# Filler matmuls, packed step places and one warm-up token less in a chunked sigmoid recurrence

## The reference, cut to what matters

```python
# x: (32, 32, 16, 25).  Three stages, each of them once:
# 1. a graph convolution with four temporal branches and a residual
# 2. attention over T*V = 400 tokens of 32 channels, per sample of the batch of 32
#    scores = exp(-(|q|^2 + |k|^2 - 2 q.k)); attn = softmax(scores); out = attn @ V, added to its input
# 3. a recurrence over the 400 tokens:
Wx = ((flat - mean) * rsqrt(var + 1e-5) * gamma + beta).reshape(B, T, H)    # H = 32
def step(yt, wx_t):
    yt = sigmoid(wx_t + yt @ V.T)            # V is orthogonal, 32 x 32
    return (yt, yt)
_, ys = scan(step, zeros(B, H), swapaxes(Wx, 0, 1))                          # 400 steps; ys is added to the input
```

## Time and profile before

| what | value |
|---|---|
| median of three runs | 237.83 us (237.7 to 238.28) |
| the profiled execution: its own time | 237.66 us |
| its span, first to last instruction | 235.8 us |
| PE busy | 199.2 us, 85% |
| ACT busy | 169.9 us, 72% |
| DVE busy | 157.7 us, 67% |
| mean granted TensorE clock | 0.956 |

### The profile page before, as it was taken

The page is one execution under the profiler, slowest core; times in us unless marked ns, Lnnn a source line. Parts: engine busy times, 40 slices in busy tenths (PEclk is TensorE's granted clock), DMA queues, the critical chain, the costliest instruction groups (busy, mean ns, idle before and its releaser), DMA issues. The chain is left out here.

```text
span 235.8 us, 3561 instructions
## 1 busy us (share of the span) xinstructions
PE 199.2 (85%) x1110; PEld 94.1 (40%) x1110; DVE 157.7 (67%) x296; ACT 169.9 (72%) x309; POOL 27.5 (12%) x44
## 2 busy tenths in 40 slices
PE   0775998898899797959989999999999998588950
PEld 0552554464465353523333343434343333245630
DVE  0417618965992992399578577777869695595880
ACT  4028179579759959797998999999899984365640
POOL 6000000054024006016100101010101000000000
PEclk9997699999999999997999999999999999889985
DMA  6940020039599709348880716162520000000016
GB/s 173 372 126 0 0 72 1 0 77 348 160 273 285 221 0 308 129 138 296 212 215 0 192 23 190 22 169 47 176 37 0 3 0 0 0 3 0 0 51 233
DMA packets 26883, 26.83 MB, mean 114 GB/s; under 512 B 1550, under 2 KB 25806, under 8 KB 26740
## 3 DMA queue, kind: packets, MB, share of 16 engines
q1 hardware_dynamic: 26868, 26.64, 38.6%
HBM read 14.74 MB, written 11.88 MB: 113 GB/s over the span
## 5 line engine op out<-in xcount | busy, mean ns | idle before, releaser
L474 ACT ACTIVATE arena<-ps 128x800 f32<-128x800 f32 (+1 forms) x56 | 44.5, 796 | 6.5 <-PE ps L980 4.9
L481 ACT ACTIVATE arena<-arena 128x800 f32<-128x800 f32 (+1 forms) x56 | 46.3, 829 | 0.0
L980 PE MATMUL ps<-qa,ka 128*128 128x400 bf16 (+1 forms) x128 | 35.8, 343 | 3.6 <-ACT arena L474 3.6
L980 PE MATMUL ps<-qb,kb 96*128 96x400 bf16 (+1 forms) x128 | 35.7, 341 | 0.0
L702 DVE TENSOR_TENSOR psum<-arena 128x400 f32<-128x400 f32 x32 | 19.6, 612 | 13.5 <-ACT arena L481 13.4
L702 DVE TENSOR_TENSOR psum<-psum,arena 128x400 f32<-128x400 f32 x32 | 19.5, 609 | 7.2 <-ACT arena L481 5.8
L1013 PE MATMUL ps<-arena,vb 128*32 128x400 f32 x192 | 21.0, 513 | 0.8 <-issue 0.8
L905 PE MATMUL ps<-arena,cst 128*128 128x400 f32 x32 | 15.7, 620 | 6.5 <-DVE arena L627 6.5
L980 PEld LDWEIGHTS ps<-qa,ka 128*128 128x128 bf16 (+1 forms) x128 | 10.4, 98 | 26.9 <-ACT arena L474 10.0
L1094 PE MATMUL ps<-yb,cst 128*128 128x160 f32 x76 | 17.2, 335 | 2.2 <-ACT yb L551 1.3
L711 DVE RECIPROCAL arena<-ps 128x400 f32<-128x400 f32 x7 | 18.6, 2651 | 0.0
(11 more groups left out here) (137 smaller groups left out, 357.4 us busy)
## 6 DMA issues: line engine op xcount, KB each, us to landing
dka<-arena SPq DMA_DIRECT2D x16, 200.0 KB, 3.1
dqa<-arena SPq DMA_DIRECT2D x16, 200.0 KB, 3.2
ka<-dka SPq DMA_DIRECT2D x8, 400.0 KB
qa<-dqa SPq DMA_DIRECT2D x8, 400.0 KB
arena<-x_tok SPq DMA_DIRECT2D x4, 400.0 KB
t<-x SPq DMA_DIRECT2D x1, 1600.0 KB, 12.1
dkb<-arena SPq DMA_DIRECT2D x8, 200.0 KB, 3.5
dqb<-arena SPq DMA_DIRECT2D x8, 200.0 KB, 4.6
```

The costliest lines, as they stand in the source:

```text
L474: nc.scalar.activation(prob[par][:, lo:hi, :], ps[:, o:o + hi - lo, 0:N], ACT.Exp, scale=2.0).then_inc(e1_done, 1)
L481: nc.scalar.activation(p, p, ACT.Exp).then_inc(p_ready, 1)
L980: last = mm_(ps[row:row + keys, bank, 0:N], kk[par][0:rows, b, o:o + keys], qq[par][0:rows, b, :], start=first, stop=not first, skip_group ...
```

## The change

Five things are changed.

1. A matmul `fill` of 256 bfloat16 columns into an unused bank (bank 3) follows every half step on TensorE, in both sweeps, and ten of them (`FILLS_FIRST`) stand between the last `prime` and the first half step.
2. Sweep 0 starts at token 1 of each chunk (`SKIP` = 1) and so takes nine steps.
3. The first of these nine has no matmul (its start state is zero), and ScalarE computes it straight from `ul` in SBUF, with `scl` and `shf` as scale and bias.
4. The steps' places are packed into banks 0 to 2 of each half (`PLACES` = 9): sweep 0 uses eight places, seeded as 3, 3 and 2; sweep 1 uses nine, and its last step takes place 0 again, seeded while the sweep runs (`last_seeds`). Six banks are primed and not eight. The signs of `tot` and `nshf` are turned (`shf`).
5. SP's loops over stores and loads are written out, and the loads of group 2 stand before the last `de` store.

```diff
-BLOCKS = ((0, 1), (1, 4), (4, 7), (7, 10))
+PLACES = 9
+SKIP = 1
+FILL = 256
+FILLS_FIRST = 10
...
-        PRIME_ORDER = (3, 7, 0, 4, 1, 5, 6, 2)
+        PRIME_ORDER = (0, 4, 1, 5, 2, 6)
+        FILL_BANK, SMALL_BANK = 3, 7
...
+        def place(sweep, s):
+            return s - SKIP - 1 if sweep == 0 else s % PLACES
...
-            with sp.Fori(1, PAIRS) as i:
+            for i in range(PAIRS - 1):
                 store(i)
-            with sp.Fori(1, PAIRS) as i:
-                for par in range(2):
-                    sp.wait_ge(s_done, UNITS * (2 * i + par - 1))
-                    load_operands(i, par)
+                store_e(i)
+                if i == 0:
+                    for par in range(2):
+                        load_operands(0, par)
+            store(PAIRS - 1)
+            load_next(1, 0)
+            store_e(PAIRS - 1)
+            load_next(1, 1)
+            for i in range(2, PAIRS):
+                for par in range(2):
+                    load_next(i, par)
...
             for h in range(2):
-                act.wait_ge(seeded[h], 1)
-                step(h, 0)
-            for s in range(1, L):
+                act.wait_ge(bn_c, 5)
+                nc.scalar.activation(y_half(h, SKIP + 1), ul[:, h, SKIP, :, :].rearrange("p g c -> p (g c)"),
+                                     ACT.Sigmoid, bias=shf, scale=scl).then_inc(y_ok[h], 1)
+            for s in range(SKIP + 1, L):
...
+            def last_seeds(base):
+                for h in range(2):
+                    dve.wait_ge(y_ok[h], base + 3)
+                    seed(h, 1, PLACES, L)
...
                 for j in range(L - 1):
+                    if seeding and j == 3:
+                        last_seeds(base)
...
+            def fill():
+                mm_(ps[:, FILL_BANK, 0:FILL], ka[0][:, 0, 0:P], ka[0][:, 0, 0:FILL], start=True, stop=True)
...
-            for bank in PRIME_ORDER[:-1]:
+            for bank in PRIME_ORDER:
                 prime(bank)
-            pe.wait_ge(bn_pe, 2)
-            prime(PRIME_ORDER[-1])
+            for _ in range(FILLS_FIRST):
+                fill()
...
+            def step(h, sweep, s):
+                mm_(step_slot(h, place(sweep, s)), c_("vT"), y_half(h, s), start=False, stop=True,
                     skip_group_check=True).then_inc(pre[h], 1)
+                fill()
```

More of the change, by code:

```diff
@@ L217, in build, with step_slot, seed_count @@
         LAST_BANKS = {G - 2: (0, 1), G - 1: (2, 3)}
-        def step_slot(h, s):
-            bank, o = (3, 0) if s == 0 else ((s - 1) // 3, SLOT * ((s - 1) % 3))
-            return ps[:, 4 * h + bank, o:o + SLOT]
-        def block_of(s):
-            return next(n for n, (lo, hi) in enumerate(BLOCKS) if lo <= s < hi)
+        def place(sweep, s):
+            return s - SKIP - 1 if sweep == 0 else s % PLACES
+        def step_slot(h, p):
+            return ps[:, 4 * h + p // 3, SLOT * (p % 3):SLOT * (p % 3 + 1)]
+        def seed_count(sweep, s):
+            return s // 3 + 1 + (PLACES // 3 + 1) * sweep - 1 if sweep else (s - SKIP - 1) // 3 + 1
         def y_half(h, s):
@@ L548, in _ @@
             nc.scalar.preload_act_table_set("sigmoid_and_others")
-            def step(h, s):
-                nc.scalar.activation(y_half(h, s + 1), step_slot(h, s), ACT.Sigmoid).then_inc(y_ok[h], 1)
+            def step(h, sweep, s):
+                nc.scalar.activation(y_half(h, s + 1), step_slot(h, place(sweep, s)), ACT.Sigmoid).then_inc(y_ok[h], 1)
             def steps(base):
@@ L571, in _ @@
                 with act.Fori(0, NC - 1) as k:
-                    steps(2 * L + L * k)
+                    steps(2 * L - SKIP + L * k)
         @block.vector
@@ L840, in _ @@
             with dve.If(dve.value_load(flag[0:1, 0:1], min_val=0, max_val=1) != 0):
-                dve.wait_ge(primed, len(PRIME_ORDER) + 1)
                 with dve.Fori(0, NC - 1) as k:
                     for h in range(2):
-                        chain(h, 2 * L + L * k)
-                        for n in range(len(BLOCKS)):
-                            seed(h, n)
+                        chain(h, 2 * L - SKIP + L * k)
+                        for lo, hi in LATER:
+                            seed(h, 1, lo, hi)
+                    last_seeds(2 * L - SKIP + L * k)
                 for h in range(2):
-                    dve.wait_ge(y_ok[h], 2 * L + L * (NC - 1))
+                    dve.wait_ge(y_ok[h], 2 * L - SKIP + L * (NC - 1))
                 dve.wait_ge(out_done, 16 * (G // OUT_G))
-                add_residual(2 * L + L * (NC - 2))
+                add_residual(2 * L - SKIP + L * (NC - 2))
         @block.tensor
@@ L1103, in steps @@
                         else:
-                            pe.wait_ge(y_ok[h], L * sweep + s)
-                        step(h, s)
-            for s in range(1, L):
+                            pe.wait_ge(y_ok[h], L * sweep - SKIP + s)
+                        step(h, 1, s)
+            for s in range(SKIP + 1, L):
                 for h in range(2):
-                    pe.wait_ge(seeded[h], block_of(s) + 1)
-                    pe.wait_ge(y_ok[h], s)
-                    step(h, s)
+                    pe.wait_ge(seeded[h], seed_count(0, s))
+                    pe.wait_ge(y_ok[h], s - SKIP)
+                    step(h, 0, s)
             steps(1)
             pe.wait_ge(cmp_c, 4)
-            mm_(ps[0:1, 7, 0:1], okc, c_("ones")[:, 0:1], start=True, stop=True).then_inc(cmp_pe, 1)
+            mm_(ps[0:1, SMALL_BANK, 0:1], okc, c_("ones")[:, 0:1], start=True, stop=True).then_inc(cmp_pe, 1)
             pe.wait_ge(flag_ok, 1)
             with pe.If(pe.value_load(flag[0:1, 0:1], min_val=0, max_val=1) != 0):
-                prime(7)
                 with pe.Fori(0, NC - 1) as k:
```

65 lines of the change are left out of this document (33 added, 32 removed).

## The result

| | before | changed |
|---|---|---|
| median of 20 executions each, same chip | 238.36 us (235.88 to 241.1) | 235.66 us (232.77 to 240.32) |
| ratio, 95% interval | | 0.987 (0.984 to 0.990) |
| the profiled execution: own time, span | 237.66, 235.8 | 235.07, 233.2 |
| mean granted clock in it | 0.956 | 0.967 |

The change is worth about 2.7 us by the medians (238.36 - 235.66), where 0.9 was forecast.

What follows compares the result with a forecast made beforehand. Taken as bound: the recurrence's latency, one half alternating matmul and sigmoid, 0.995 us a step. Own time 237.66 - 0.75 (start) - 0.1 (SP's queue) = 236.8; the median 0.17 above, less rounding: 236.9 us, range 236.0 to 237.8.

Steps and rivals of the forecast that it cites:

- term 2: SP's queue, at ScalarE's two waits for the last `dqb` store: written-out stores land slightly earlier, -0.1 us.
- the row nearest to the new form is not shorter: SP's stores: pair 0, already written out, took 7.33 us against 7.15 for looped pair 2, so little gain was booked.
- one of the two waits vanishes: ScalarE's waits for `dqb`: one disappears, -1.2 us; part of the more-is-gained rival, 236.0 us, 13%.
- term 1: Start of the recurrence: a step less (0.995), of which fills take back 0.25; -0.75 us.
- I take the phase that the trace shows: Start of the recurrence: clock assumed to rise at about 208.23, as in the one profiled execution; basis of -0.75 us.
- the ten fills booked as a cost: Between primes and first half step: ten fills set the start; they and the fill between halves take back 0.25 us.
- the prediction's bound of 1.7: Start of the recurrence: if the clock rises early, VectorE's seeds decide and the gain is up to -1.7 us.
- Rival 4: Recurrence steps: the fill's weight load is not hidden, steps take 1.17 us, 18 steps add 3.1; 240.0 us, 12%.
- Rival 2: Start of the recurrence: ten fills and some first steps run at half clock, leaving 0.16 of the gain; 237.6 us, 15%.
- the loop fills cost nothing at the upper level: Both sweeps: 36 fills stand in TensorE's idle time behind half steps, costed at nothing; cover 0.16 us a gap.
- the late seeds of step 9: Sweep 1 on VectorE: two seeds, 0.88 us, fit into 1.6 us of idle time; cost 0.
- nine steps meet the bound without further sweeps: Sweep 0: nine steps shrink a difference to 2^-18, just the comparison's bound; further sweeps, 388 us, given under 1%.

Runs made afterwards that it cites:

- e9: Changed kernel with 14 unused semaphore increments in SP's queue between pair 2's two sets of stores, delaying its last store; 237.14 us, ratio 0.988 to the kernel before.
- e7: Changed kernel with the last `de` store put back ahead of the loads of group 2; 236.98 us, ratio 0.995 to the kernel before.
- e11: Kernel before with 26 fills in TensorE's idle time ahead of the small matmul, nothing else changed; 238.17 us, ratio 0.998.
- e2: Changed kernel with the old SP queue of the kernel before; 236.77 us, ratio 0.993 to the kernel before.
- e1: Kernel before with the new written-out SP program alone; 237.36 us, ratio 0.990.
- e10: Changed kernel with three semaphore increments moved from the head of SP's program to GpSimd; 235.03 us, ratio 0.989 to the kernel before.
- e6: Changed kernel with 26 fills ahead of the small matmul instead of ten behind the primes, and the usual fills behind half steps; 235.13 us, ratio 0.987.
- e13: Changed kernel with SP's program three increments shorter and without any fill; 236.96 us, ratio 0.999 to the kernel before.
- e16: Kernel before with the written-out SP program, three increments shorter, and its old recurrence without fills; 236.76 us, ratio 0.993.
- e14: Changed kernel with SP's program three increments shorter and only the ten fills ahead of the first half step; 235.67 us, ratio 0.989 to the kernel before.
- e8: Changed kernel once more, unedited, beside three other runs on their chip; 236.72 us, ratio 0.994 to the kernel before.
- e5: Changed kernel without the ten fills ahead of the first half step, keeping those behind half steps; 237.14 us, ratio 0.996 to the kernel before.
- e3: Changed kernel without any fill, the missing step and packed places kept; 236.66 us, ratio 0.996 to the kernel before.
- e12: Changed kernel with 26 fills ahead of the small matmul instead of ten behind the primes, and SP's program three increments shorter; 235.4 us, ratio 0.990.
- e4: Changed kernel with the ten fills ahead of the first half step but none behind half steps; 235.92 us, ratio 0.989 to the kernel before.
- e15: Second run of the changed kernel with all fills and SP's program three increments shorter; 236.12 us, ratio 0.991 to the kernel before.

## Why the prediction was wrong in size

**SP's queue (term 2, forecast -0.1): the step that failed is "the row nearest to the new form is not shorter".** Pair 0's 7.33 us was nearest in form but had other traffic beside it; pair 2 written out took 6.47. And the value isn't one for one: 0.77 us of earlier issue got the store past a code fetch and landed it 1.98 earlier. e9 shows it by undoing the issue time, pair 3 of the kernel before by a store as late without a fetch, e7 that the moved loads have no part. A is shorter by 0.84 in the pair of traces: 0.15 ahead of pair 2's first store, 1.28 from there to pair 3's, and 0.58 lost again up to the second wait. It is shorter by 0.7 against e11 and by 1.6 against e2, of which 0.5 lie where e2's clock was low; e1's median gives 0.9. The rival "one of the two waits vanishes" came true at the first wait, and part of it was lost at the second, where SP stands still for 0.43 us. That this stop is itself a wait for code is likely, since it moved when the program got shorter (e10) and longer (e9), but no run shows it.

**The start (term 1, forecast -0.75): the steps that failed are "I take the phase that the trace shows" and the ten fills booked as a cost.** One trace's clock phase isn't the kernel's. With the low stretch over the primes, B is 13.07 or 13.21 with the old steps and 12.08, 12.20 or 12.35 with the new ones: -0.7 to -1.1, so the size worked out for that phase holds. Where the clock did not fall at all (e6, e10), B is 1.46 under before's, near the prediction's bound of 1.7. But B was 14.81 for the old steps in e1 and 13.73 for the new ones in four traces of seven that had both kinds of fill. The sum's 0.25 for ten fills was right as occupancy of TensorE, and missed their other side: without them, with two primes fewer, the clock is often low far into sweep 0, and the missing step is given back (e13 against e16: +0.2, where -1.0 was to be had). With them it comes back (e13 to e14: -1.3).

**Rival 4, the fill's load not hidden, falls.** Steps are 1.00 apart, sweep 1 takes as long as before, and a 98 ns load of the full array stands under a running matmul. The Trainium skill, "TensorE: Matmul & The Clock Gate", Part 3, under what overlaps and what doesn't, has a load overlap matmuls only when it goes to other row groups, and so would have had it wait for them; this case's trace disagrees, at 218.46.

**Rival 2, the low stretch later,** is what the changed kernel's own trace shows (rows above), and e2's, e7's and e8's. Its price was wrong: 0.16 of term 1 was to be left, and B grew by 0.66. The fills took their 2.13, and the first half step started 4.93 us behind the small matmul, where the price has 209.44 - 204.64 = 4.80. But from there to h1's sigmoid of step 2 it took 1.53, and the price kept the 0.84 of the upper level: that the half steps behind the fills run at the lower level too was left out, 0.69 of the 0.82 missed. It was also set against a fixed before, and the old steps can be slow too (14.81 in e1 and e11).

**Right as forecast:** the loop fills cost nothing at the upper level (at the lower they cost 0.14 a step, e5); the late seeds of step 9 delay nothing; the moved loads are worth nothing; the tail is unchanged; nine steps meet the bound without further sweeps.

**Where the 2.7 went.** By parts: SP -0.9 (e1), the steps -1.5 (e2), together 2.4. The mean of the kernel before beside the experiments is 238.33 (94 executions), that of the changed one 236.03 (26, the result's and e8's), -2.3. The traces account for A's -0.7 to -0.84 and, with B's mean over traces (13.7 for the old steps in three, 13.0 for the new with all fills in seven), -0.7. The remaining 0.8 to 0.9 isn't placed. Against e2's A it would be nothing, and a part of it may be SP's: all three traces with the old queue have a low stretch of the clock at 105 to 114 us, none of the eight with the new one has (the changed kernel, e1, e3 to e8), and e9, e10, e12 and e13 have it again. It may also be chance: of these 94 executions of the kernel before none had a mean granted clock over 0.976, of the changed kernel's first 20 six had 0.984 or more, and of e8's six none. Of the kernels with ten fills, the four traces with 6.8 us at the lower level are those in which the clock had fallen 0.4 to 0.5 us ahead of the small matmul (changed, e2, e7, e8); where it fell later, between 0.3 ahead and 0.6 behind (e4, e9, e14, e15), it was 3.4, and in e10 it did not fall. What sets that moment was not found.

**The best version.** e10 with either set of fills (e10, e14, e15: 235.03, 235.67, 236.12) and e6 (235.13) beat the kernel before, but can't be told from the changed kernel; the short program takes 0.6 us off A, of which about 0.3 is left in the own time.

## What to carry to other kernels

A kernel that passes an idle gap on TensorE can have several clock histories, not one: compare stages over several traces before costing anything at one phase, and don't cut a step or a warm-up matmul ahead of a sparse chain without keeping TensorE full until the clock is up. A filler in such a gap is worth what it does to the clock, and fillers between steps that already run at the upper level are worth nothing; at the lower level they lengthen the steps. An issue queue's time is worth nothing where the landing doesn't follow it (pair 3's +8.9 from either issue), and more than itself where it gets a transfer past something that comes at its own time (here a fetch of code), so look at landings and not at issues.

## What the runs showed of the hardware that was not expected

- Engines' code arrives in 8 and 16 KB fetches over the same DMA engines as the data; one of 16 KB, 1.5 us long, stood between a store's issue and its landing (+10.82 against +8.84 us, and +8.98 for a store issued as late without one).
- The loop form of SP's program cost 0.7 us per twelve store issues at pair 2 (7.15 against 6.47) and 0.55 at pair 3 (7.12 against 6.57).
- An idle gap of 2.8 us on TensorE was passed with the clock at 1.00 in one execution (e10) and with a fall in it in others (the changed kernel, 0.5 us ahead of its end).
- A sigmoid of 128x160 float32 from SBUF with scale and bias took 514 ns (line 581 above), from PSUM without them 303 (line 570). It isn't on the path here.
- Two executions of the kernel before took 640.53 and 382.72 us. The first is 402 more than usual, about 39 sweeps of 10.3; the second fits no count of sweeps that the kernel can take. Neither is explained.
